# Value projection for four pairs of heads at once, softmax reciprocals by log and exponential, norms two tiles at a time, routing steps moved

## What is computed

```
lat = layer_norm(layernorm(x));  ctx = layer_norm(context)        # (8,512,256), (8,1024,256)
q = lat @ Wq                     # 16 heads of 64
k, v = split(ctx @ Wkv)          # 16 heads of 64;  k = apply_rope(k, cos, sin)
attn = softmax(clip(q k^T / 8, -11, 11))
x1 = x + tanh(g_xattn) * ((attn v) @ Wo + bo)
xf = layernorm(x1)
scores = sigmoid(xf @ router_w.T)   # 64 experts in 8 groups; best 4 groups, best 8 experts of them
routed = sum over the 8 chosen experts of gate * (relu(xf @ up)^2 @ down)
out = x1 + tanh(g_ffn) * (routed + shared expert of xf)
```

## Time and profile before

| | us |
|---|---|
| median of 3 runs | 2636.36 |
| their range | 2633.79 to 2646.41 |
| the profiled execution | 2636.81 |
| span in its trace | 2634.7 |
| attention, batches 0 to 7 | from 56.8 to about 1967 |

### The profile page before, as it was taken

The page is one execution under the profiler, slowest core; times in us unless marked ns, Lnnn a source line. Parts: engine busy times, 40 slices in busy tenths (PEclk is TensorE's granted clock), DMA queues, the critical chain, the costliest instruction groups (busy, mean ns, idle before and its releaser), DMA issues. The chain is left out here.

```text
span 2634.7 us, 43493 instructions
## 1 busy us (share of the span) xinstructions
PE 2331.4 (88%) x12227; PEld 1360.2 (52%) x12227; DVE 2171.2 (82%) x3638; ACT 1420.3 (54%) x2520; POOL 1789.0 (68%) x1723
## 2 busy tenths in 40 slices
PE   2999999899989998998999899989987968999980
PEld 2554545454444544454545445444543646987870
DVE  4888788898888898898888898988897676688884
ACT  3666556565555555555665556555552323666660
POOL 3777676488858876886787588758874730077776
PEclk9999999899999999999999899999997988999995
DMA  8434334011102111120111112111114408799994
GB/s 298 155 124 159 112 112 162 29 58 55 63 29 78 57 51 44 57 69 31 65 53 54 40 57 77 53 42 55 56 49 147 157 16 291 235 329 322 332 322 138
DMA packets 166488, 305.11 MB, mean 116 GB/s; under 512 B 20914, under 2 KB 100210, under 8 KB 166002
## 3 DMA queue, kind: packets, MB, share of 16 engines
q1 hardware_dynamic: 138162, 234.88, 26.2%
q0 software_dynamic: 24576, 67.14, 7.7%
q10 hardware_dynamic: 3520, 0.27, 0.1%
HBM read 172.46 MB, written 129.76 MB: 115 GB/s over the span
## 5 line engine op out<-in xcount | busy, mean ns | idle before, releaser
L1124 POOL TENSOR_SCALAR e<-e 128x1024 f32<-128x1024 f32 x520 | 639.8, 1230 | 406.1 <-ACT e L1029 379.5
L1029 ACT ACTIVATE e<-scores 128x1024 f32<-128x1024 f32 x520 | 533.4, 1026 | 530.5 <-PE scores L897 509.0
L1297 DVE TENSOR_TENSOR e_sum<-e_sum,e 128x1024 f32<-128x1024 f32 x391 | 585.9, 1498 | 47.5 <-POOL e L1124 44.9
L952 PE MATMUL ps_o<-e,v 128*64 128x512 f32 x2088 | 567.7, 622 | 1.6 <-POOL e L1124 1.6
L897 PE MATMUL scores<-q_t,k_t 64*128 64x512 f32 x3120 | 505.3, 429 | 15.5 <-DVE affine L1242 14.2
L897 PEld LDWEIGHTS scores<-q_t,k_t 64*128 64x128 f32 x3120 | 255.0, 186 | 377.1 <-issue 255.4
L1831 POOL DMA_INDIRECT more<-results_in_blocks,index x256 | 245.4, 959 | 210.2 <-DMA results_in_blocks<-more 129.6
L1043 ACT ACTIVATE k_sw<-ps_k 32x512 f32<-32x512 f32 x512 | 301.3, 588 | 114.6 <-PE ps_k L928 110.0
L1105 POOL DMA_INDIRECT rows_in_blocks<-room,a_r_index_now x192 | 247.9, 1291 | 50.9 <-issue 50.1
L913 PE MATMUL ps_v<-wv,ctx_t 128*128 128x256 f32 x1536 | 252.5, 301 | 0.0
L928 PE MATMUL ps_k<-ctx_t,wqk 128*128 128x512 f32 x768 | 218.6, 422 | 33.8 <-DVE q_t L1276 33.5
(11 more groups left out here) (287 smaller groups left out, 3606.3 us busy)
## 6 DMA issues: line engine op xcount, KB each, us to landing
rows_in_blocks<-room SPq DMA_DIRECT2D x16, 2560.0 KB, 9.8
x_nat<-rows_in_blocks SPq DMA_DIRECT2D x160, 256.0 KB
results_in_blocks<-more SPq DMA_DIRECT2D x80, 512.0 KB
wqk<-wqk_pairs SPq DMA_DIRECT2D x65, 512.0 KB, 3.5
wv<-wv_doubles SPq DMA_DIRECT2D x33, 512.0 KB, 3.3
wo<-in_L_xattn_Wo SPq DMA_DIRECT2D x66, 128.0 KB, 3.4
x_nat<-in_ctx SPq DMA_DIRECT2D x64, 128.0 KB, 3.2
down_all<-in_L_ffn_down_w SPq DMA_DIRECT2D x16, 512.0 KB, 8.6
```

Source lines behind the costliest of these rows:

```text
L952: mm = pe.matmul(ps_o[hh * DH:(hh + 1) * DH, :], v[:, tile, buf, hh * DH:(hh + 1) * DH], e[:, tile % 4, hh * N:(hh + 1) * N], start=(tile ...
L1029: act.activation(e[:, c % 4], scores[:, c % 2], ACT.Exp, scale=SCALE).then_inc(s_exp, 1)
L1124: pool.tensor_scalar(e[:, c % 4], e[:, c % 4], EXP_HI, EXP_LO, ALU.min, ALU.max).then_inc(s_clip, 1)
L1297: dve.tensor_tensor(total, e[:, 0] if c == 2 else total, e[:, tile % 4], ALU.add).then_inc(s_sum, 1)
```

## The change

- The weights of the values are stored for four pairs (512 columns). In pairs 0 and 4 the tiles 0 to 3 are projected in slots 3, 5, 6, 7, in pairs 1 and 5 the tiles 4 to 7 in slots 1, 3, 5, 7; pairs 2, 3, 6 and 7 have none. `v` has four places a tile instead of three.
- `e_sum` has one buffer.
- The reciprocal: ACT computes r = exp(-ln(y)) in slot 2, DVE computes o_n = y*r and then (o_n - 2)*r in slot 3. That is the negative of the refined reciprocal, and the gate's sign is turned. POOL's first product stands behind the clip of slot 3.
- ACT's table set with both log and exponential is asked for at the start and again after each tanh of the routing.
- Batches 1 to 7: the next batch's context comes by one DMA, and two tiles at a time are made ready in pairs 1 to 6 (latents in 1 and 2), statistics in slot 0, roots in slot 1, normalisation in slot 6. Batch 0 stays as it was.
- Routing: group steps move from pairs 5 and 6 to earlier slots, `overflow` goes to slot 1 of pair 7, and the last three of six `number_blocks`, `place` and `cross` go to slots 1 and 2 of the next batch's pair 0; `finish_slots` has five parts, in slots 1, 2, 4, 6, 7. The scatters start at slot 0 of pair 1 instead of slot 7 of pair 0 and end at slot 1 of pair 7. `crossed` shares memory with `cmp_a`.

The core of the diff:

```diff
-        wv = sb("wv", [P, 2, C2, 2 * P], FR)
+        wv = sb("wv", [P, 2, C2, 4 * P], FR)
-        v = sb("v", [P, ST, 3, P])
+        v = sb("v", [P, ST, 4, P])
-        e_sum = sb("e_sum", [P, 2, CH])
+        e_sum = sb("e_sum", [P, CH])
+        FINISH = (1, 2, 4, 6, 7)
-        def value_tile(p, m, c):
-
-            if p in (None, 0):
-                return c if m % 2 == 0 else None
-            if m % 2:
-                return {3: 0, 5: 1, 6: 2, 7: 3}.get(c) if p < PAIRS - 1 else None
-            return {1: 4, 3: 5, 5: 6, 7: 7}.get(c)
+        def value_tile(m, c):
+
+            if m == 0:
+                return {3: 0, 5: 1, 6: 2, 7: 3}.get(c)
+            if m == 1:
+                return {1: 4, 3: 5, 5: 6, 7: 7}.get(c)
+            return None
...
PE
-                            mm = pe.matmul(ps_v[:, 0:2 * P], ctx_t[:, a, cc, tile * P:(tile + 1) * P], wv[:, bb, cc],
+                            mm = pe.matmul(ps_v[:], ctx_t[:, a, cc, tile * P:(tile + 1) * P], wv[:, bb, cc],
+                    if m == 2 and c == 1:
+                        pe.wait_ge(s_v, 1 + (g // 4 + 1) * 8)
...
ACT
+            act.preload_act_table_set("natural_log_exp_and_others")
...
                     router.tanh(act, b - 1, y_flat)
+                    act.preload_act_table_set("natural_log_exp_and_others")
...
+                if c == 2:
+                    act.wait_ge(s_den, 1 + g + 1)
+                    act.activation(r_den[:], y_flat, ACT.Ln).then_inc(s_log, 1)
+                    act.wait_ge(s_log, g + 1)
+                    act.activation(r_den[:], r_den[:], ACT.Exp, scale=-1.0).then_inc(s_seed, 1)
...
POOL
-                if c == 3:
-                    pool.wait_ge(s_rec, g * 2 + 1)
-                    pool.wait_ge(s_oraw, g + 1)
-                    pool.tensor_tensor(o_n[:, 0:D], o_raw[:, 0:D], r_den[:, 0:D], ALU.mult).then_inc(s_on, 1)
                 if attend:
                     pool.wait_ge(s_exp, 2 + g * 8 + c + 1)
                     pool.sem_inc(s_seen, 1)
                     pool.tensor_scalar(e[:, c % 4], e[:, c % 4], EXP_HI, EXP_LO, ALU.min, ALU.max).then_inc(s_clip, 1)
+                if c == 3:
+                    pool.wait_ge(s_rec, g + 1)
+                    pool.wait_ge(s_oraw, g + 1)
+                    pool.tensor_tensor(o_n[:, 0:D], o_raw[:, 0:D], r_den[:, 0:D], ALU.mult).then_inc(s_on, 1)
...
DVE
-                if c in (2, 3):
-                    half = slice((c - 2) * D, (c - 1) * D)
-                    dve.wait_ge(s_den, 1 + g + 1)
-                    dve.reciprocal(r_den[:, half], y_flat[:, half]).then_inc(s_rec, 1)
+                if c == 3:
+                    dve.wait_ge(s_seed, g + 1)
+                    dve.tensor_tensor(o_n[:], y_flat, r_den[:], ALU.mult).then_inc(s_part, 1)
+                    dve.wait_ge(s_part, g + 1)
+                    dve.scalar_tensor_tensor(out=r_den[:], in0=o_n[:], scalar=2.0, in1=r_den[:],
+                                             op0=ALU.subtract, op1=ALU.mult).then_inc(s_rec, 1)
...
+                    if 1 <= p <= GROUPS_OF_ROWS and c in (0, 6):
+                        k = p - 1
...
+                        if c == 0:
+                            norms.moments_of(dve, rows, first, units_written(b) + k)
+                        else:
+                            norms.normalise(dve, rows, places, first, units_written(b) + k)
...
+                if not isinstance(b, int) and p == 0 and c in FINISH:
+                    finish_slots(b - 2, FINISH.index(c))
...
-                if (p, c) == (7, 0):
+                if (p, c) == (7, 1):
                     router.overflow(dve)
-                if (p, c) == (7, 1):
                     router.count_blocks(dve)
+                if (p, c) == (7, 2):
                     router.number_blocks(dve, range(0, 3))
-                if (p, c) == (7, 4):
-                    router.number_blocks(dve, range(3, 6))
-                if (p, c) == (7, 5):
-                    router.place(dve)
-                if (p, c) == (7, 6):
-                    router.cross(dve)
-                    crossing[0] = router.k
+                    numbered[0] = router.k
```

171 lines of the change are left out of this document (98 added, 73 removed).

## The result

The changed kernel takes 2622.24 us (median of five, 2619.38 to 2624.40) against 2640.39 (2633.79 to 2646.41) for the kernel before, measured in turn: a ratio of 0.993 with an interval of 0.991 to 0.995, 18 us. The forecast was 2566, 72 us less. The profiled execution took 2619.68 us with a span of 2617.9.

The account below looks back on a forecast made before the run. PE's own stream was taken to bound pairs 0, 1, 3 and 4, with some 17 us of waits per batch, half at the boundary. From 2636.8: -35 boundaries, -34 and -8 pairs, +5 clock = -72, taken as 2566; range 2525 to 2632.

Parts of the forecast that it names:

- Boundary (-35): Between batches: 2.7 us DVE tail plus 5.1 to first scores, 7.8 instead of 13.8; six times, 35 us less.
- Values: Value projection on PE: 1.58 us per wide tile, 25.3 us a batch instead of 28; heavy pairs 29.4, light 23.1.
- Reciprocal: DVE's reciprocal 1.8 us less per pair; in light pairs POOL's product ends at 14.7, PE wants it at 15.1.
- Rival 1: Reciprocal chain late every step, DVE and POOL slowing each other at SBUF: 45 to 60 us lost, 2610 to 2625; chance 0.16.
- The 0.5 us for small misses: Light pairs: 0.5 us added each for small misses in the 28 not otherwise priced.
- Clock: PE's granted clock: 5 us added over six batches for pair 2's stall, and 0.8 us in each pair 0.
- Pair 7 (23.9): Pair 7, batches 2 to 7: query's low part ends at 12.8, PE arrives at 12.5; 23.9 us, before 26.1.
- Base: Starting length of the pairs in batches 2 to 7, read from batch 4: 228.6 us, falling to 222.9.
- Tables: ACT's table loads: two in pair 4 of seven batches, 1.28 us each, hidden from PE, no cost.
- POOL's queue in pair 2: Pair 2: POOL's product ends near 19.5 us, PE arrives at 15.1, a 4.4 us stall; pair 28.1, before 30.1.
- pairs 1, 3 and 5 of batch 4: Pair lengths forecast at 29.4, 24.2 and 30.0 us, before 26.6, 27.1 and 28.3.
- Pairs 0, 4 and 6: Pair lengths forecast at 30.2, 31.3 and 25.8 us, before 31.2, 28.8 and 30.4.

## Why the prediction came out as it did

**Boundary (-35): nearly right.** It is 8.7 us for 7.8. The term of 2.7 for DVE's tail was 3.3, as DVE's last sum takes 2.06 us beside POOL, and 1.05 us lie between DVE's two pieces of work, for 0.8 gained on the affine steps. The base was 13.3 on average over the six boundaries instead of 13.8.

**Values: the tile right, the worth wrong.** 1.60 us for 1.58, and heavy pairs at 29.4 as worked out. But the saving counts only where PE is the bound. The prediction said that DVE and POOL lose 3.5 us of cover in pairs 2, 3 and 6, and then priced that in pair 2 alone. Pair 6 now waits 1.3 us a batch for the product, pair 3 0.8 for the sum, batch 0's pairs grew by 4.5 us in all and batch 1's gained 1 us instead of 8.

**Reciprocal: a failing step.** "It holds by 0.4 us where DVE and POOL are not behind" gave POOL's product 0.9 us (13.8 to 14.7), near the 0.72 of the earlier trace rows. That row is the product when it reads SBUF first. The change takes away the PSUM reader that stood beside it and releases the product and DVE's addition at one moment, so that it costs 1.58 us in most steps. The extra 0.7 us are more than the 0.4 of slack. Rival 1 had this, priced at 45 to 60 us with a chance of 0.16. The missing 57 us are close to that, but not all of them are this mechanism, so that rival 1's time is right in part by luck: outside pair 2 PE waits 15 us for the product in batches 2 to 7; in batches 0 and 1 it is 7.5 us, of which the forecast had 2.5, in pair 2 of batch 1. Together some 20 us. Moving the product to DVE brought 22. The 9 for DVE's sum may belong to it too; no run tells. The 0.5 us for small misses, meant for 28 light pairs, stands in the sum for pairs 3 and 6 only, 6 us over batches 2 to 7. In pair 2 of batches 2 to 7 PE waits 24 us for POOL, where the walk through that pair had 26.

**Clock: the other failing step, a term of the right kind and a third of its size.** I added 5 us over six batches for pair 2, and 0.8 a batch in pair 0 as half of its old loss. Measured is 67.9 us of PE's work at half clock in the pairs of batches 2 to 7, costing half of that, 34 us, where the sum had 10. That is 24 us, as large a miss as the product's. Pair 0's loss did not halve: PE stands still less at the boundary, and 27.5 us of pair 0 are at half clock where it was 23.0. In each batch it costs 2.3 us in pair 0, 2.5 in pair 2 and 0.9 in pair 7. Taking the stall away (product ahead of the clip) took the half clock out of pairs 2 and 7 and left pair 0's.

**Pair 7 (23.9): wrong by 2.6 on average, by 3.1 in batch 4.** DVE's block counts take 3.43 + 1.58 us, the 4.9 of the forecast, but they begin only 8.3 us into the pair and have an addition between them, so that the low part ends at 14.9 and not at 12.8. PE arrives at 13.0 (forecast 12.5) and waits 2.01 us instead of 0.3. Most of the rest is the half clock behind that wait.

**Base.** The prediction took 228.6 us for the pairs from batch 4; the mean over batches 2 to 7 is 230.2. That hid 10 us of the miss: against measured lengths, the forecast of 222.9 is 9 us a batch too low, 54 us, and not 44.

**Tables, POOL's queue in pair 2, pairs 1, 3 and 5 of batch 4: right**, as the rows above show. Pairs 0, 4 and 6 are 1.5, 1.3 and 1.0 us over on average; in pair 0 it is the clock, in pairs 4 and 6 PE waits 1.0 and 1.3 us a batch for POOL's product or DVE's sum.

Had the two engines' reading of SBUF been priced from rows, the forecast would have lain nearer to rival 1. The rows for it were there: before the change, too, POOL's second product has a median of 1.58 us beside the addition (58 of 66), and its first one 0.73 beside the reciprocal.

**Left open.** No run gives `e_sum` its second buffer back; DVE waits in only 3 places, 4.9 us in all, for the matmul that frees the one it has. What the moved routing is worth alone (20 or 5 us) is open too. That the product is slow because of DVE's addition is shown by which instructions overlap, by order of start and by the product's removal from POOL; no run doubled or removed the addition alone. The 22 us of moving the product to DVE hold both halves of its delay, the slow reading and the clip ahead of it (9 us when that alone is undone). When exactly the granted clock falls is only read from rows: it fell in pair 2 of all six batches, with a stall of 3.08 us, and in pair 7 of three of the six, with a wait of 2.01 to 2.05 us that all six have. It stayed at 1.00 in pair 2 with the product ahead of the clip, where PE stands still for 0.80 and then 1.85 us in the same place.

## What to carry to other kernels

Before trusting a duration in a chain with little slack, look at what the other engine does beside it: a cheaper instruction may take away the cover under which its neighbour was fast. Price a new stall of PE with the half clock that follows it, not with its length alone. And when parts lean on each other, undoing them one by one tells which of them is a precondition (here the reciprocal for the moved routing), not what each is worth.

## What the hardware showed unexpectedly

- A stall of 3.08 us in the midst of dense work was followed by 6.8 us at half clock in batch 4, which cost 3 us more. A wait of 2.01 to 2.05 us was followed by 3.4 us at half clock in three of six batches and by none in the others.
- POOL's product of 128x256 takes 0.72 us when it starts first and 1.58 beside a DVE addition with two SBUF inputs that started first; DVE's addition takes 1.22 alone, and 1.76 and 2.06 in the two places above where it met POOL.
- Moving that product to DVE (128x512 at once, 85 us for 66) took 204 us of busy time from POOL and gave DVE 23.
- ACT's tables were exchanged twice a batch for 1.28 us each, and PE waited for none of these loads.
